# Selective scan beside attention: the products with C move from GpSimd to VectorE

## What is computed

```python
def step(state, inp):                      # over the 512 tokens
    d, b, c, u = inp
    dA = jnp.exp(d[..., None] * A)         # (batch, 512 channels, 16 states)
    state = state * dA + (d * u)[..., None] * b[:, None, :]
    y = jnp.einsum('bdn,bn->bd', state, c)
    return (state, y)
```

## Time and the profile before

| | |
|---|---|
| median of 3 runs | 2012.26 us (2010.86 to 2016.66) |
| the profiled execution: device time | 2007.29 us |
| its span from first to last instruction | 2005.5 us |
| mean granted TensorE clock | 0.887 of full |
| first and last scan (L1066) start at | 331.9 us and 1400.0 us |
| busy over the span: PE, DVE, ACT, POOL | 73%, 69%, 52%, 62% |

### The profile page before, as it was taken

How to read it: one execution, slowest core, us unless ns; L and a number is a source line. 1 busy time by engine, 2 the same in 40 slices (tenths; PEclk the granted TensorE clock), 3 DMA queues, 4 the chain that set the end, 5 groups by cost and what they waited for, 6 DMA issues and landing times. The chain is left out here.

```text
span 2005.5 us, 22953 instructions
## 1 busy us (share of the span) xinstructions
PE 1472.1 (73%) x7296; PEld 1145.4 (57%) x7296; DVE 1393.0 (69%) x2406; ACT 1050.0 (52%) x2381; POOL 1246.8 (62%) x602
## 2 busy tenths in 40 slices
PE   2333227898797989878987979897167877878776
PEld 0111015787676777767776767786145656656554
DVE  3755444877777769758777767878446858768587
ACT  2554313665555546546654545666335737556374
POOL 1221122988787898878888858989556526255263
PEclk8766558999898989989998979999669999999999
DMA  4324463324434342362344343322342121121211
GB/s 139 127 102 169 169 196 124 95 64 121 132 127 126 108 134 68 122 189 76 104 119 133 105 148 106 106 64 79 142 121 74 37 88 46 47 79 37 84 47 37
DMA packets 125439, 210.07 MB, mean 105 GB/s; under 512 B 11204, under 2 KB 60872, under 8 KB 123160
## 3 DMA queue, kind: packets, MB, share of 16 engines
q1 hardware_dynamic: 125336, 208.81, 32.8%
HBM read 158.05 MB, written 50.72 MB: 104 GB/s over the span
## 5 line engine op out<-in xcount | busy, mean ns | idle before, releaser
L1150 POOL TENSOR_TENSOR state<-state,Cn 128x1024 f32<-128x1024 f32 x128 | 309.8, 2420 | 171.7 <-DVE state L1066 171.7
L1156 POOL TENSOR_TENSOR y_sb<-y_sb,state 128x1024 f32<-128x1024 f32 x128 | 306.2, 2392 | 33.4 <-DMA y_sb<-scratch_y 23.3
L1139 POOL TENSOR_TENSOR state<-dtu_sb,Bn 128x1024 f32<-128x1024 f32 x128 | 307.7, 2404 | 28.7 <-DMA Bn<-scratch_bc 25.3
L1066 DVE TENSOR_TENSOR_SCAN state<-dA,state 128x512 f32<-128x512 f32 x256 | 310.5, 1213 | 3.7 <-ACT dA L912 2.2
L1676 POOL TENSOR_TENSOR act_buf<-act_buf,wb 128x512 f32<-128x512 f32 x128 | 179.8, 1405 | 214.4 <-ACT act_buf L1626 214.0
L553 PE MATMUL psP<-x_hi,w_hi 128*128 128x512 f32 x384 | 174.1, 453 | 161.0 <-DMA x_lo<-scratch_xs 74.7
L912 ACT ACTIVATE dA<-dt_sb,negA 128x512 f32<-128x512 f32 x256 | 177.3, 692 | 119.5 <-DVE state L1066 91.8
L553 PEld LDWEIGHTS psP<-x_hi,w_hi 128*128 128x128 f32 x384 | 80.7, 210 | 187.9 <-issue 147.4
L554 PE MATMUL psP<-x_lo,w_hi 128*128 128x512 f32 x384 | 164.1, 427 | 0.0
L555 PE MATMUL psP<-x_hi,w_lo 128*128 128x512 f32 x384 | 163.5, 426 | 0.0
L1729 DVE TENSOR_TENSOR act_buf<-psGU,act_buf 128x512 f32<-128x512 f32 x136 | 93.3, 686 | 93.3 <-POOL act_buf L1676 79.3
(11 more groups left out here) (220 smaller groups left out, 4587.7 us busy)
## 6 DMA issues: line engine op xcount, KB each, us to landing
x_hi<-scratch_xs SPq DMA_DIRECT2D x32, 512.0 KB, 6.6
x_lo<-scratch_xs SPq DMA_DIRECT2D x32, 512.0 KB, 7.6
Bn<-scratch_bc SPq DMA_DIRECT2D x64, 256.0 KB, 3.5
Cn<-scratch_bc SPq DMA_DIRECT2D x64, 256.0 KB, 3.5
scratch_acc<-acc_sb SPq DMA_DIRECT2D x64, 256.0 KB, 3.8
wb<-scratch_wT SPq DMA_DIRECT2D x64, 256.0 KB, 3.2
acc_sb<-scratch_acc SPq DMA_DIRECT2D x48, 256.0 KB, 2.6
w_stage<-in_w SPq DMA_DIRECT2D x32, 256.0 KB, 4.5
```

The costliest lines, as they stand in the source:

```text
L1066: nc.vector.tensor_tensor_scan(row, dA[:, :], row, 0.0, ALU.mult, ALU.add) \
L1139: nc.gpsimd.tensor_tensor(st[:, k % 4], dtu[:, 2 * h:2 * h + 2, :], Bn[:, state % NB, :].unsqueeze(1).broadcast_to([P, 2, T]), ALU.mult).t ...
L1150: nc.gpsimd.tensor_tensor(st[:, k % 4], st[:, k % 4], Cn[:, state % NB, :].unsqueeze(1).broadcast_to([P, 2, T]), ALU.mult).then_inc(S["gat ...
L1156: nc.gpsimd.tensor_tensor(y[:, 2 * h:2 * h + 2, :], y[:, 2 * h:2 * h + 2, :], st[:, k % 4], ALU.add).then_inc(S["piece_done"], 1)
```

## The change

DVE writes the recurrence over the decay factors, in the PSUM tile dA, and then multiplies what stands there by C and writes the product into the `state` buffer. It waits for its own scan (`scan_step`) before the product. `scan_done`, which releases ACT's next decay and POOL, is now raised by the product. POOL keeps the drive and the addition into y; a wait on `piece_done` keeps two additions into the same half of y apart. SP's load of the next C waits for DVE's last product with it.

```diff
@@ SP, end of step p
                     if p + 2 < NSTATE:
-                        sp.wait_ge(S["gated"], 2 * p + 2)
+                        sp.wait_ge(S["scan_done"], 4 * p + 4)
                         load_c(p + 2)
@@ DVE, scan(i)
                     row = st[:, i // 2 % 4, i % 2, :]
-                    nc.vector.tensor_tensor_scan(row, dA[:, :], row, 0.0, ALU.mult, ALU.add) \
+
+                    state = i // CT
+                    nc.vector.tensor_tensor_scan(dA[:, :], dA[:, :], row, 0.0, ALU.mult, ALU.add) \
+                        .then_inc(S["scan_step"], 1)
+                    dve.wait_ge(S[f"c_loaded{state % NB}"], 16 * (state // NB + 1))
+                    dve.wait_ge(S["scan_step"], i + 1)
+                    nc.vector.tensor_tensor(row, dA[:, :], Cn[:, state % NB, :], ALU.mult) \
                         .then_inc(S["scan_done"], 1)
@@ POOL, loop over k
                     pool.wait_ge(S["scan_done"], 2 * k + 2)
-                    pool.wait_ge(S[f"c_loaded{state % NB}"], 16 * (state // NB + 1))
-                    nc.gpsimd.tensor_tensor(st[:, k % 4], st[:, k % 4],
-                                            Cn[:, state % NB, :].unsqueeze(1).broadcast_to([P, 2, T]),
-                                            ALU.mult).then_inc(S["gated"], 1)
                     if r == 0:
                         pool.wait_ge(S[f"y_loaded{h}"], 16 * (b + 1))
-                    pool.wait_ge(S["gated"], k + 1)
+                    if k >= 2:
+                        pool.wait_ge(S["piece_done"], k - 1)
                     nc.gpsimd.tensor_tensor(y[:, 2 * h:2 * h + 2, :], y[:, 2 * h:2 * h + 2, :],
                                             st[:, k % 4], ALU.add).then_inc(S["piece_done"], 1)
                     if k + 3 < NDRIVE:
                         drive(k + 3)
```

More of the change, by code:

```diff
@@ L543, in attend_and_scan @@
                  "b_loaded0", "b_loaded1", "c_loaded0", "c_loaded1",
-                 "dA_done", "dbu_done", "scan_done", "gated", "piece_done")
+                 "dA_done", "dbu_done", "scan_step", "scan_done", "piece_done")
         sems = [ctx.enter_context(nc.semaphore(n)) for n in names]
```

## The result

The median of four runs is 2071.4 us (2067.6 to 2072.2), that of before beside them 2014.5 us: the ratio is 1.028, 95% interval 1.0256 to 1.0304. The profiled execution took 2071.45 us, its span is 2069.7 us. I had said slower, 2043 us, between 1998 and 2075.

A forecast was written before the change was run, and what follows sets the result against it. DVE was to become the bound in plain steps: taken 834 + 184 - 8 = 1010 us, plus 95 idle, a stretch of 1105 instead of 1071. That made 2041 profiled, 2043 us as median, range 1998 to 2075.

The forecast's parts named there:

- a step lasts what DVE's work lasts: Plain steps: DVE becomes the bound there and its work sets the step's length; 34 us more in all, chance 0.58.
- price of a piece: DVE, scan and product: 0.72 us more for each of 256 pieces, 184 us in all, between 154 and 210.
- Shared reads: DVE's weight splits L976 and L981: less stretched beside a less busy POOL, 8 us off, between 0 and 15.
- Idle time, 95 us: DVE's idle time left in the scans' stretch after the change, 95 us in all, where it was 237.
- (a): DVE's short waits that come from ACT's order stay: about 1.7 us in 4 steps, 26 us in all.
- (d): DVE's idle time at the start and end of the stretch: 3 us.
- (c): Three ends of a sequence: pT_lo waits 2.5 us instead of 8.8, the x load 6.3 instead of 10.4; 26 us.
- (b): Plain loads of x: DVE waits 3.3 us for kT_lo instead of 9.3, twelve times, 40 us.
- Faster by x: Rival: loads of x shrink and DVE's waits absorb most products, if idle stays under 61 us; 1991 us, chance 0.16.
- No change, as the own wait is free: Rival: DVE's wait for its own scan costs nothing, DVE taken for 979 us; time 2010, chance 0.11.
- PE loses its clock: Rival: PE waits for DVE each half step, its clock falls from 0.93 to 0.80; 2063 to 2080 us, chance 0.15.
- Such waits are under 1 us each: Reason against the PE clock rival: PE's many small waits for DVE each last under 1 us.

The follow-up runs named there:

- e10: e1 with the product, in two of four pieces, put between the reciprocal of `combine` and what follows: 2049.6 us.
- e1: The changed kernel with DVE's wait for the load of C moved from ahead of the product to ahead of the scan: 2053.0 us.
- e2: The kernel before with the multiplication by C left out on both POOL and DVE: 1939.3 us.
- e4: The changed kernel with the scan writing into SBUF as before, so that DVE's product reads two SBUF operands: 2142.8 us.

## Why the prediction was right, and where its terms were off

**Direction and mechanism: right in the main.** DVE became the fullest engine, the idle time that it had was not where the products are, x came in time in plain steps. Of the signs that I had named, the product's group, POOL's 602 us (590 forecast), x issued within 1 us of its last use where neither weights nor the end of a sequence come, and PE's wait of 40.3 us (at the upper end of 30 to 40) came. Three did not: the product starts 1.33 us after its scan, not 1.25, DVE's waits are 107 us, not 95, and first and last scan lie 59 us further apart, not 34. And "a step lasts what DVE's work lasts" was too simple, as e10 shows: 22 us less of DVE's work gave 3. The size was off by 28 us: 2071 instead of 2043, inside the range and 6 us above my forecast's own range (2018 to 2065). In the profiled executions, which I had put at 2041, it is 30 us: 13 by the time that DVE is taken (1023 us, not 1010), nearly all of it the price of a piece, 12 by idle time, 5 after the last scan.

**The price of a piece, 0.72 us: too low.** It was 1.25 + 0.60 - 1.13. Measured, as means over 256 pieces from the starts of DVE's instructions: 1.325 + 0.616 - 1.173 = 0.768, so 197 us instead of 184. The scan before was dearer than the one row that I had read for it (a mean of 1.173, not 1.13: -11 us; where the next instruction waits for another engine, the scan holds DVE to its end, 1.21), the product a little dearer (+4), and the scan with its gap 1.325 instead of 1.25 (+19). This last is the split-off wait, which I had not counted and which no row of before shows; e1 measures it by itself, 18.5 us. This was the largest single miss.

**Shared reads, 8 us off: about right in sum, wrong in place.** Taken rose by 189 us against 197 from the products. The durations of L981 and L976 after (ns: min, median, max) show why:

```profile
L981 DVE SCALAR_TENSOR_TENSOR ow_lo<-w_stage,subln,ow_hi x16: 743/746/752, 324.0 to 1245.3; 128x512 fp32r<-128x512 f32 x16
...
L976 DVE SCALAR_TENSOR_TENSOR w_lo<-w_stage,w_hi x32: 679/682/2492, 287.0 to 1159.4; 128x512 fp32r<-128x512 f32 x32
```
```profile
L976 DVE SCALAR_TENSOR_TENSOR w_lo<-w_stage,w_hi 128x512 fp32r<-128x512 f32 x32 | 43.9, 1374 | 0.7 <-ACT w_hi L821 0.7
```

L981 lost all its stretches, but L976, on which I had built the term, keeps a mean of 1374 ns (1328 before), and in the stretch every second one (12 of 24) takes 2.4 to 2.5 us, about as long as one of POOL's remaining operations (2385 and 2429 ns). That they wait for one of these fits, but no run isolates it.

**Idle time, 95 us: 107 measured.** By its parts: (a) and (d), 29 us of short waits, are 34 (qT_lo 17.4, negmax 6.3, v_lo 6.0, dA 3.2, ow_lo 1.0). The pT_lo part of (c) is right: 7.9 us in all against 7.5. kT_lo is 64.0 against 59, but otherwise spread than in (b) and (c). The timelines at a new set of weights and at the first end of a sequence, SP and DVE:

```profile
540.76 0.63 SPq L589 DMA_DIRECT2D x_hi<-scratch_xs  x1
...
556.67 0.75 DVE L996 SCALAR_TENSOR_TENSOR kT_lo<-psP,qk_bias,kT_hi 128x512 fp32r<-128x512 f32 x1 [6.65 <-ACT kT_hi L844]
...
604.43 0.33 SPq L598 DMA_DIRECT2D Bn<-scratch_bc  x1
...
612.11 0.69 DVE L1027 TENSOR_TENSOR pT_lo<-psS,pT_hi 128x512 fp32r<-128x512 f32 x1 [2.48 <-ACT pT_hi L868]
...
633.34 0.75 DVE L996 SCALAR_TENSOR_TENSOR kT_lo<-psP,qk_bias,kT_hi 128x512 fp32r<-128x512 f32 x1 [7.56 <-ACT kT_hi L844]
```

Where neither weights nor the end of a sequence come, a load of x leaves 0 to 4.95 us of waiting where I had forecast 3.3 (six of nine leave less than 1). At three iterations with new weights it leaves 6.4 to 6.7: PE had ended its last use at 536.6, and SP issued x at 540.8, 4 us late (4.6 us at the same place before). Its queue had left `load_b` at 528.2 and then waited until 534.7 for a lower part of the weights. Such waits were 7.1 us in all before:

```profile
SPq L574 <- DVE w_lo L976: 45.9, 9, 5.8
```

That a slower DVE makes SP wait I had left out; I had let only POOL do that. At the ends of a sequence it is 7.6 to 9.5 instead of 6.3.

**After the last scan: 5 us more**, where I had none. The code is the same there. The trace has PE at the lower level of its clock for 109 us of that part instead of 97; at half the clock this would make up to 6 us, an estimate from these two times that no run isolates.

**The rivals.** *Faster by x* fails on its condition: idle would have had to be under 1071 - 1023 = 48 us. But it had more in it than I gave it: POOL's relief is worth 75 us (e2). *No change, as the own wait is free* is refuted as to the engine by the spacings above, 1.25 us with one wait and 1.13 without; as to the end of the kernel, e1 refutes it for the split-off wait alone. That the product could run without a wait for its scan was not tried, as it would be a race. *PE loses its clock* is not what happened over the stretch (0.93 as before), but it shows in places. PE at one such place: two waits, then a projection, and the windows (PE clock is the third last column) of these 4.6 us and of 7 us ahead:

```profile
1007.96 0.66 PE L777 MATMUL psO<-ident,head 128*128 128x128 f32 x4 [1.45 <-ACT head L895]
...
1010.87 0.80 PE L553 MATMUL psP<-x_hi,w_hi 128*128 128x512 f32 x1 [1.15 <-DVE qT_lo L996]
1011.46 0.63 PE L554 MATMUL psP<-x_lo,w_hi 128*128 128x512 f32 x1
```
```profile
1011.50:1016.10 4.60, 4.60 (x12) 3.61 (x11) 3.23 (x7) 1.50 (x5) 3.44 (x2) 0.50 0.42 114
1000.00:1007.00 7.00, 6.51 (x31) 4.91 (x29) 6.72 (x15) 3.91 (x14) 4.44 (x2) 1.00 0.00 0
```

The granted clock falls from the upper of its two levels (2.4 GHz) to the lower (1.2), and the projection's twelve matmuls take 5.3 us from the first's start to the next operation (1010.87 to 1016.16); then qT_lo waits 2.21 us on DVE. In e1, after waits of 0.36 us for the head and 0.22 at the same projection, the matmuls follow each other at the full clock:

```profile
1010.65 0.50 PE L553 MATMUL psP<-x_hi,w_hi 128*128 128x512 f32 x1 [0.22 <-DVE qT_lo L996]
1010.98 0.40 PE L554 MATMUL psP<-x_lo,w_hi 128*128 128x512 f32 x1
```

"Such waits are under 1 us each" was my reason against this rival, and it was wrong in this place: 1.45 and 1.15 us. Over the kernel it is small: the mean of all 384 such matmuls (L554) is 435 ns against 427 before, and of the whole stretch 164 us lie at the lower level instead of 146, which at half the clock is at most 9 us of PE's work, an estimate from these two times.

## What to carry to other kernels

Price an instruction that waits for the one ahead on its engine by the distance between starts, see whether a wait has been split off between the two, and put waits that have long been met ahead of the first one. Before moving work off an engine because others wait for it, look at which queue carries that lateness: here the order of one DMA queue gave 68 us, and 82 with dt, without moving any arithmetic, where moving the arithmetic lost 57. And test the two halves of such a move by themselves (less work here, more work there): 75 us gained and 132 lost say at once that the receiving engine is the wrong one.

## What the runs showed of the hardware that I had not expected

- Two waits ahead of a DVE instruction that depends on the one before it cost 0.07 us more than one (1.325 against 1.257 us from scan to product in e1), though one semaphore has long been raised: one of the waits stands in the trace as an instruction of its own (L1071), which starts 0.04 us after the scan's end.
- An independent DVE instruction starts 1.13 us after a scan of 1.21 us, one that waits for the scan 1.25 us after (e10).
- One more SBUF operand makes a 128x512 DVE product 1.07 us on average instead of 0.69 (690 to 693 ns in the change), up to 2.76, beside a POOL that is busy half of the time, and POOL's operation 2567 ns instead of 2429 (e4).
- PE waited 1.45 and 1.15 us within 3 us, and the 4.6 us behind went at half the clock, while the stretch's mean showed nothing (0.93 before and after).
